# One-core language-model tower: the opening reordered, from the weight loads to the first attention heads

## The chip, the cores and the metric

The kernel runs on one core of a Trainium2 chip. The core has five engines that run side by side and meet only at semaphores: TensorE (PE in the rows, its weight loads PEld), VectorE (DVE), ScalarE (ACT), GpSimd (POOL) and SyncE (SP), which here only starts transfers. The metric is the device time of one execution in microseconds, the median of several runs. The kernel before took 1006.28 us (median of three, 1006.02 to 1006.45).

## The reference, cut to what matters

`x` holds 8 x 512 token ids below 2048. Everything is float32.

```python
h = gelu(codebook[x] @ W1 + b1) @ W2 + b2            # 256 -> 1024 -> 256
n = layernorm(h);  x_tok, x_pos = n[..., :128], n[..., 128:]
q, k, v = x_pos @ Wq, x_pos @ Wk, x_tok @ Wv         # 16 query heads, 4 key/value heads of 64
q = rotate(q, q_phase_angle)                         # one fixed angle for each head
att = q @ k^T / 8 + exp(alibi_log_slopes) * (i - j)  # causal
att = exp(att - max) / (1 + sum(exp(att - max)))
h = h + (att @ v) @ Wo
m = layernorm(h)
h = h + gelu((m @ U1) @ V1 + b1f) @ U2 @ V2 + b2f    # low rank 64
```

## The kernel before

**First stage, `token_table`.** The first expression depends on the token id alone. So it is computed once for each of the 2048 codebook rows, in four chunks of 512 (`NC = 4`), and kept in DRAM as a table of 640 columns: 256 of `h`, 128 of the normalised second half (the input of queries and keys), 256 of values. Each chunk is 8 steps; step n is numbered over all 32, `i` is the chunk and `m` the step in it. Every float32 matrix is split into a high and a low part, and a product is three matmuls. In a step TensorE makes `first_product(n)` (six matmuls of 512 columns) and `second_product(n - 2)` (twelve of 256). ScalarE does the gelu and the high part, VectorE the low part. `first_product(n)` needs the gelu of step n-2, and `second_product(n)` the low part of step n.

The order on every engine is written out by hand. At the start SP loads chunk 0 of the codebook, W1 in two halves of 128 rows (with the tiny `b1_col` between them), W2 in four parts, `b2_row`, and the other chunks. ScalarE makes the two high parts of W1, then two sines and an exponential (`sin_t`, `half`, `slope`), then meets the gelus. Its functions come in tables, and each change of function other than Copy is preceded by a load (ACT_TABLE_LOAD). VectorE prepares the angles (`ang`) ahead of the low parts of W1.

A chunk's rows are finished while the next one runs: `keep_rows` (VectorE, at m = 1) adds the bias into the tile `made`, `norm_front` (m = 2) takes the statistics, GpSimd raises to the power -1/2, `norm_back` (m = 4) writes the normalised columns of `made` and the normalised token half (`tokens`, in the buffer named scratch). TensorE turns those tokens (`turn_tokens`) at m = `TURN_AT` = 5, and multiplies them with Wv at m = 7. SP stores the rows twice: into `early_rows` (384 columns, for the first batch entry alone) and into `table`. The stage ends with a barrier of all engines once `early_rows` of the last chunk has landed.

**Second stage, `layer`.** It walks over 128 heads (8 batch entries of 16) in slots `s`, with 16 more slots to drain. At its head TensorE turns and multiplies the last chunk's tokens, and GpSimd gathers the first batch entry's rows from `early_rows` and, once the last values are stored, its values from `early_values`. The whole rows of batch entry b+1 are gathered from `table` by `gather(b + 1)` at slot 1 of entry b. Each gather is four indirect DMAs that GpSimd itself issues, before it goes on.

In a slot: TensorE makes the scores of head s in three units (`scores(s, 0..2)`: query block 3; 2 and 0; 1) into two PSUM banks taken in turn. VectorE adds the bias and takes the least (`least_of`, four instructions), ScalarE takes the exponentials (`exps`, four), VectorE takes the reciprocal of the sums (`invert`), GpSimd scales the probabilities (`normalize`, four instructions). Two slots later TensorE turns them (`turn`), ScalarE moves the turned tile to SBUF (`move`), and TensorE multiplies with the values for two heads at a time (`values`). Queries of two heads, keys of four and the inputs of the next batch entry are further products, listed by `first(s)`, and all go through one PSUM bank (`a_bank`) in turn: a product may start when VectorE has made the low part (`low`) of the one before. `first(s)` stands, on TensorE, between `scores(s, 1)` and `scores(s, 2)`; on ScalarE ahead of the exponentials of head s; on VectorE ahead of the fourth `least_of`. `second(s)` stands at the end of the slot on each of them.

## Time and profile before

| | |
|---|---|
| median of three runs | 1006.28 us |
| the profiled execution | 1006.18 us |
| its span in the trace | 1004.4 us |
| mean granted TensorE clock | 0.965 |
| PE / ACT / POOL / DVE busy | 87% / 72% / 63% / 61% |
| first stage, up to the barrier | about 0 to 126.8 us |
| first head's scores begin | 141.7 us |

The profiled execution lasted 1.8 us longer than its span, which is the time around the first and the last recorded instruction. TensorE is the busiest engine overall, but a share over the whole span says nothing of the opening; for that the trace is read stretch by stretch. Times of rows are microseconds from the start of the span.

### The profile page before, as it was taken

The page shows a single profiled execution, that of the slowest core. Times are in us where ns is not written, and L with a number is a line of the kernel's source. Part 1 is how long each engine was busy: PE and PEld are TensorE (multiplying, and loading weights), DVE is VectorE, ACT ScalarE, POOL GpSimd, SP SyncE. Part 2 cuts the span into 40 slices and gives each one's busy share as a digit, 9 for nine tenths or more (in the row PEclk, how much of TensorE's full clock was granted, in tenths as well). Part 3 has the DMA queues.
Part 4 walks back from the last instruction along what each step waited for, and adds up shares of the span by engine and source line. Part 5 has one row for each costly group of instructions (what it writes and reads, how often), then busy time and mean ns, then how long its engine had stood idle before and what let it go on. Part 6 is the DMA issues. An engine that isn't in the chain of part 4 may idle for free.

```text
span 1004.4 us, 16876 instructions
## 1 busy us (share of the span) xinstructions
PE 875.8 (87%) x5552; PEld 676.1 (67%) x5552; DVE 611.1 (61%) x1896; ACT 723.1 (72%) x1600; POOL 630.9 (63%) x600
## 2 busy tenths in 40 slices
PE   6999657999988998889888998899889988998876
PEld 5888545677865786568656875677567855786563
DVE  4565525777684658475847684767566765668321
ACT  6654236998678768886888687877787787868713
POOL 6000038999684878478857874887669775768520
PEclk9999867999999999999999999999999999999997
DMA  9232341001000200020001100010001000000000
GB/s 260 33 105 105 133 129 53 1 1 54 2 1 1 74 1 1 1 60 16 1 1 35 41 1 1 22 54 1 1 22 53 2 1 22 1 2 1 1 21 21
DMA packets 21206, 33.55 MB, mean 33 GB/s; under 512 B 2513, under 2 KB 18033, under 8 KB 21121
## 3 DMA queue, kind: packets, MB, share of 16 engines
q1 hardware_dynamic: 17360, 19.01, 5.8%
q0 software_dynamic: 3760, 13.48, 4.9%
q8 instruction: 45, 0.74, 0.3%
q14 instruction: 41, 0.33, 0.1%
HBM read 17.80 MB, written 14.68 MB: 32 GB/s over the span
## 4 chain that ended last, share of the span: by engine, by line
PE 51%; DVE 14%; ACT 12%; issue 8%; POOL 1%; DMA 0%; DVEq 0%; ACTq 0%; POOLq 0%
PE ps L972 15%; PE ps L1097 10%; PE ps L1081 8%; ACT probs L747 6%; PE ps L1069 5%; DVE probs L870 5%; PE ps L1070 4%; PE ps L1049 3%; ACT turned_sb L754 3%; PE ps L1043 2%; DVE q_both L887 1%; DVE xn L859 1%; PE ps L1044 1%; DVE sums L877 1%; ACT q_both L764 1%
## 5 line engine op out<-in xcount | busy, mean ns | idle before, releaser
L712 POOL TENSOR_SCALAR probs<-probs,sums 128x512 f32<-128x512 f32 (+3 forms) x512 | 546.4, 1085 | 200.7 <-DVE sums L879 200.3
L870 DVE CUSTOM_DVE_ANT_0 probs<-ps,causal,slope 128x512 f32<-128x512 f32 (+3 forms) x512 | 259.4, 547 | 81.0 <-PE ps L1070 79.1
L747 ACT ACTIVATE probs<-probs,least 128x512 f32<-128x512 f32 (+3 forms) x512 | 282.0, 553 | 23.3 <-DVE least L870 18.8
L754 ACT ACTIVATE turned_sb<-ps 128x1280 f32<-128x1280 f32 x128 | 157.4, 1230 | 89.4 <-PE ps L1081 89.4
L1069 PE MATMUL ps<-k_hi,q_both 128*128 128x512 f32 (+3 forms) x512 | 185.9, 363 | 33.4 <-DVE least L870 31.8
L1097 PE MATMUL ps<-turned_sb,token_rows 128*64 128x512 f32 (+3 forms) x1024 | 152.0, 438 | 29.6 <-ACT turned_sb L754 29.6
L1081 PE MATMUL ps<-ident,probs 128*128 128x128 f32 x1280 | 166.0, 278 | 4.0 <-POOL probs L712 4.0
L1070 PE MATMUL ps<-k_lo,q_both 128*128 128x512 f32 (+3 forms) x512 | 154.5, 327 | 0.0
L1097 PEld LDWEIGHTS ps<-turned_sb,token_rows 128*64 128x64 f32 x1024 | 74.7, 136 | 116.8 <-issue 100.4
L1081 PEld LDWEIGHTS ps<-ident,probs 128*128 128x128 f32 x1280 | 147.8, 144 | 7.0 <-POOL probs L712 5.4
L1069 PEld LDWEIGHTS ps<-k_hi,q_both 128*128 128x128 f32 x512 | 98.2, 192 | 78.8 <-DVE least L870 54.8
L1070 PEld LDWEIGHTS ps<-k_lo,q_both 128*128 128x128 f32 x512 | 98.9, 193 | 4.5
L747 ACT ACTIVATION_READ_ACCUMULATOR probs<-probs,least 128x1 f32 x512 | 96.1, 188 | 0.0
L887 DVE TENSOR_TENSOR q_both<-ps,q_both 64x512 fp32r<-64x512 f32 x128 | 88.1, 689 | 11.9 <-ACT q_both L764 8.7
L764 ACT ACTIVATE q_both<-ps 64x512 fp32r<-64x512 f32 x128 | 75.4, 589 | 23.6 <-PE ps L972 22.1
L251 POOL TENSOR_TENSOR row_guess<-row_var,row_power 128x4 f32<-128x4 f32 x4 | 4.1, 1026 | 97.0 <-DVE row_var L350 97.0
L972 PE MATMUL ps<-wo_lo,o_hi 128*128 128x256 f32 x224 | 63.3, 282 | 0.0
L972 PE MATMUL ps<-wo_hi,o_hi 128*128 128x256 f32 x224 | 63.2, 282 | 0.0
L972 PE MATMUL ps<-wo_hi,o_lo 128*128 128x256 f32 x224 | 62.9, 281 | 0.0
L922 DVE TENSOR_TENSOR o_lo<-ps,o_hi 128x512 fp32r<-128x512 f32 x64 | 44.2, 691 | 23.3 <-ACT o_hi L796 23.1
L913 DVE TENSOR_TENSOR y_lo<-ps,y_hi 128x512 fp32r<-128x512 f32 x8 | 5.5, 692 | 81.1 <-ACT y_hi L790 81.1
L786 ACT ACTIVATE ff<-ps,c_col 128x512 f32<-128x512 f32 x64 | 40.7, 685 | 18.0 <-PE ps L1044 17.9
(191 smaller groups left out, 1446.6 us busy)
## 6 DMA issues: line engine op xcount, KB each, us to landing
out_dram<-token_rows SPq DMA_DIRECT2D x7, 512.0 KB, 2.9
early_rows<-made SPq DMA_DIRECT2D x4, 768.0 KB, 3.6
token_table<-made SPq DMA_DIRECT2D x4, 768.0 KB, 5.3
rows<-in_L_tok_codebook_dram SPq DMA_DIRECT2D x4, 512.0 KB, 8.0
early_values<-xn SPq DMA_DIRECT2D x4, 512.0 KB, 3.0
token_table<-xn SPq DMA_DIRECT2D x4, 512.0 KB, 4.4
w_f<-in_L_tok_W_dram SPq DMA_DIRECT2D x2, 512.0 KB, 6.3
w_f<-in_L_tok_W_dram SPq DMA_DIRECT2D x4, 256.0 KB, 8.1
```

What stands on the lines that cost most here:

```text
L712: ins = pool.tensor_scalar(at, at, recip[:, s % P_RING, q:q + 1], None, ALU.mult)
L747: act.activation(at, at, ACT.Exp, bias=least[:, s % P_RING, q:q + 1], scale=-1.0, accum_out=sums[:, s % P_RING, q:q + 1]).then_inc(exped, 1)
L754: act.activation(turned_sb[:, s % 2, :], turn_ps, ACT.Copy).then_inc(moved, 1)
L764: act.activation(q_both[at, s % 4, :], a_of("q", n, 0)[at, :], ACT.Copy).then_inc(q_high, 1)
L870: dve.tensor_tensor_reduce(out=probs[:, s % P_RING, at], in0=bank(unit % 2)[:, UNIT_AT[q]:UNIT_AT[q] + P * (q + 1)], in1=causal[:, at], sc ...
L887: dve.tensor_tensor(q_both[to, s % 4, :], a_of("q", n, 0)[at, :], q_both[at, s % 4, :].bitcast(F32), ALU.subtract).then_inc(q_low, 1)
L922: dve.tensor_tensor(o_lo[:, p % O_RING, :], o_bank, o_hi[:, p % O_RING, :].bitcast(F32), ALU.subtract)\
L972: mm = pe.matmul(dst, w, x, start=n == 0, stop=n == len(parts) - 1)
L1069: pe.matmul(dst, w, k_hi[:, slot, 0:P * (q + 1)], start=True, stop=False)
L1070: mm = pe.matmul(dst, w, k_lo[:, slot, 0:P * (q + 1)], start=False, stop=True)
L1081: mm = pe.transpose(turn_ps[:, K_AT[k] + P * (q - k):K_AT[k] + P * (q - k + 1)], probs[:, s % P_RING, Q_AT[q] + P * k:Q_AT[q] + P * (k + 1 ...
L1097: mm = pe.matmul(o_bank[rows, P * k:T], v_rows[:, b % 3, k, n // REP * D:(n // REP + 1) * D], turned_sb[:, (s + e) % 2, K_AT[k]:K_AT[k] + ...
```

## The change

Six things are done. W1 is loaded and split in four parts, first the left 512 columns of both row halves, then the right 512. The preparation of the angles and the two sines and exponential move behind W1 (VectorE) and to step 5 (ScalarE). `turn_tokens` goes from m = 5 to m = 6. The store into `early_rows` becomes two, 256 columns when `keep_rows` is done and 128 when `norm_back` is. `gather(1)` is issued before the first `normalize`, and ScalarE takes one exponential of one column (`spare`) at the head of the second stage. For slots 0 and 1 the query and key products stand in `second(s)` instead of `first(s)`, and their low parts one slot later on VectorE.

```diff
-    TURN_AT, VALUES_AT = 5, 7
+    TURN_AT, VALUES_AT = 6, 7
...
+    def w1_part(n):
+
+        return n % KD, slice(n // KD * HID // 2, (n // KD + 1) * HID // 2)
...
-            for k in range(KD):
-                sp.dma_start(w1_f[:, k, :], g["W1"][k * P:(k + 1) * P, :]).then_inc(w1_in[k], 16)
-                if k == 0:
+            for n in range(2 * KD):
+                k, cols = w1_part(n)
+                sp.dma_start(w1_f[:, k, cols], g["W1"][k * P:(k + 1) * P, cols]).then_inc(w1_in[n], 16)
+                if n == 1:
                     sp.dma_start(b1_col[:, :], ...)
...
+                sp.wait_ge(row_kept, 2 * i + 2)
+                sp.dma_start(of_chunk(g["early_rows"])[:, :, 0:DIM], made[:, :, 0:DIM]).then_inc(early_in, 16)
                 sp.wait_ge(pos_normed, i + 1)
-                sp.dma_start(of_chunk(g["early_rows"]), made[:, :, :]).then_inc(early_in, 16)
+                sp.dma_start(of_chunk(g["early_rows"])[:, :, DIM:DIM + P], made[:, :, DIM:DIM + P]).then_inc(early_in, 16)
...
             for n in range(STEPS):
                 i, m = divmod(n, KH)
+                if n == 5:
+                    act.wait_ge(trig_in, 1)
+                    act.activation(sin_t[:, :], ang[:, :], ACT.Sin).then_inc(trig_out, 1)
+                    act.activation(half[:, :], ang[:, :], ACT.Sin, scale=0.5).then_inc(trig_out, 1)
+                    act.activation(slope[:, :], ls[:, :], ACT.Exp).then_inc(trig_out, 1)
...
-                    if n == 0:
-                        pe.wait_ge(w1_low, k + 1)
+                    if n == 0 or n == KH // 2:
+                        pe.wait_ge(w1_low, n // (KH // 2) * KD + k + 1)
...
+EARLY = 2
+def queries_and_keys(s):
...
 def first(s):
     i, j = divmod(s, HEADS)
-    out = []
-    if s % 2 == 0 and s // 2 + 1 < ALL // 2:
-        out.append(("q", s // 2 + 1, 0))
-    if s % 4 == 1 and (s + 3) // 4 < ALL // REP:
-        out.append(("k", (s + 3) // 4, 0))
+    out = [] if s < EARLY else queries_and_keys(s)
...
 def second(s):
-    out = []
+    out = queries_and_keys(s) if s < EARLY else []
...
             gather_first(slice(DIM + P, ROW), g["early_values"], first_values_in)
+            gather(1)
...
-                if i + 1 < B and j == 1:
+                if i >= 1 and i + 1 < B and j == 1:
                     gather(i + 1)
...
+            act.activation(spare[:, :], ident[:, 0:1], ACT.Exp)
             act.wait_ge(tok_full, 1)
...
+                if 1 <= s <= EARLY:
+                    for use in queries_and_keys(s - 1):
+                        low(*use)
                 for use in first(s):
                     low(*use)
```

ScalarE at the very start, before: the names w1_hi and w2_hi are high parts of the weights, hid the gelu's output, ang and ls the angles and log slopes.

```order
L280 ACTIVATE w1_hi<-w1_f 128x1024 [waits w1_in0]
L280 ACTIVATE w1_hi<-w1_f 128x1024 [waits w1_in1]
L282 ACT_TABLE_LOAD
L282 ACTIVATE sin_t<-ang 128x16 [waits trig_in]
L283 ACTIVATE half<-ang 128x16
L284 ACT_TABLE_LOAD
L284 ACTIVATE slope<-ls 128x16
L289 ACTIVATE w2_hi<-w2_f 128x512 [waits w2_in0]
L295 ACT_TABLE_LOAD [waits hid_full]
L295 ACTIVATE hid<-ps,b1_col 128x512 [waits b_in]
```

The same place in the changed kernel:

```order
L289 ACTIVATE w1_hi<-w1_f 128x512 [waits w1_in0]
L289 ACTIVATE w1_hi<-w1_f 128x512 [waits w1_in1]
L289 ACTIVATE w1_hi<-w1_f 128x512 [waits w1_in2]
L289 ACTIVATE w1_hi<-w1_f 128x512 [waits w1_in3]
L299 ACTIVATE w2_hi<-w2_f 128x512 [waits w2_in0]
L305 ACT_TABLE_LOAD [waits hid_full]
L305 ACTIVATE hid<-ps,b1_col 128x512 [waits b_in]
```

Two table loads and three small functions left this place. They stand ahead of the gelu of step 5 now, and a third load stands there too, since the gelu's table must come back.

GpSimd at the head of the second stage, before: token_rows are the gathered rows, probs the probabilities of a head.

```order
L717 DMA token_rows<-early_rows,idx 128x384 x4
L717 DMA token_rows<-early_values,idx 128x256 [waits values_in]
L717 DMA token_rows<-early_values,idx 128x256 x3
L712 TENSOR_SCALAR probs<-probs,sums 128x512 [waits recip_done,start]
L712 TENSOR_SCALAR probs<-probs,sums 128x384
L712 TENSOR_SCALAR probs<-probs,sums 128x128
L712 TENSOR_SCALAR probs<-probs,sums 128x256
L700 DMA token_rows<-token_table,idx 128x640 [waits right_in,left_in]
L700 DMA token_rows<-token_table,idx 128x640 x3
L712 TENSOR_SCALAR probs<-probs,sums 128x512 [waits recip_done]
```

And in the changed kernel:

```order
L736 DMA token_rows<-early_rows,idx 128x384 x4
L736 DMA token_rows<-early_values,idx 128x256 [waits values_in]
L736 DMA token_rows<-early_values,idx 128x256 x3
L719 DMA token_rows<-token_table,idx 128x640 [waits right_in,left_in]
L719 DMA token_rows<-token_table,idx 128x640 x3
L731 TENSOR_SCALAR probs<-probs,sums 128x512 [waits recip_done,start]
L731 TENSOR_SCALAR probs<-probs,sums 128x384
```

The four gathers of the second batch entry went from between the first and second head's scaling to ahead of both.

VectorE in the first heads, before: the ISA rows that write probs and least are `least_of`, q_both is the low part of two heads' queries, k_lo that of the keys, sums the reciprocal.

```order
L870 ISA probs,least<-ps,causal,slope 128x128 [waits scored]
L870 ISA least 128x1
L887 TENSOR_TENSOR q_both<-ps,q_both 64x512 [waits q_high] x2
L870 ISA probs,least<-ps,causal,slope 128x256 [waits scored]
L870 ISA least 128x1
L877 TENSOR_SCALAR sums<-sums 128x4 [waits exped]
L879 RECIPROCAL sums<-sums 128x4 [waits v_step]
L870 ISA probs,least<-ps,causal,slope 128x512 [waits scored]
```

And in the changed kernel, up to the query's low part, from the same `least_of` of head 0 on:

```order
L892 ISA probs,least<-ps,causal,slope 128x128 [waits scored]
L892 ISA least 128x1
L892 ISA probs,least<-ps,causal,slope 128x256 [waits scored]
L892 ISA least 128x1
L899 TENSOR_SCALAR sums<-sums 128x4 [waits exped]
L901 RECIPROCAL sums<-sums 128x4 [waits v_step]
L892 ISA probs,least<-ps,causal,slope 128x512 [waits scored]
L892 ISA least 128x1
L892 ISA probs,least<-ps,causal,slope 128x384 [waits scored]
...
L909 TENSOR_TENSOR q_both<-ps,q_both 64x512 [waits q_high] x2
```

The low part of the next queries went from ahead of head 0's fourth `least_of` to behind head 1's third. In the same way k_lo went from head 1's slot to behind the third `least_of` of head 2, where the low part of the queries after that follows it at once.

## Rows read from the trace of the kernel before

**Rows 1.** Stretch: us; busy of PE, PEld, DVE, ACT, POOL; granted clock; DMA share

```profile
16.80:116.80 100.00, 96.98 (x637) 87.07 (x636) 58.61 (x136) 55.30 (x88) 5.93 (x6) 1.00 0.35 100
```

**Rows 2.** Waits of TensorE from 16.8 to 116.8: us in total, times, longest

```profile
PE ps L495 <- DVE scratch L365: 2.6, 3, 0.9
```

**Rows 3.** Timeline of the start: start, us, instruction [idle before <-releaser]

```profile
6.97 0.94 SPq L194 DMA_DIRECT2D b_row<-in_L_tok_b_dram  x1
...
7.36 1.05 ACT L280 ACTIVATE w_hi<-w_f 128x1024 fp32r<-128x1024 f32 x1
9.90 1.06 ACT L280 ACTIVATE w_hi<-w_f 128x1024 fp32r<-128x1024 f32 x1 [1.49 <-DMA w_f<-in_L_tok_W_dram]
10.97 1.28 ACT L282 ACT_TABLE_LOAD   x1
...
15.95 0.69 ACT L295 ACTIVATE hid<-ps,b_col 128x512 f32<-128x512 f32 x1
...
7.50 0.69 DVE L324 TENSOR_TENSOR ct_lo<-ps,ct_hi 128x512 fp32r<-128x512 f32 x1 [0.16 <-ACT ct_hi L260]
...
10.18 2.35 DVE L385 TENSOR_TENSOR w_lo<-w_f,w_hi 128x1024 fp32r<-128x1024 f32 x2
...
11.55 0.77 PE L469 MATMUL ps<-ct_hi,w_hi 128*128 128x512 f32 x1 [4.72 <-DVE w_lo L385]
...
16.80 0.42 PE L469 MATMUL ps<-ct_hi,w_hi 128*128 128x512 f32 x1
```

**Rows 4.** DMA issues: out<-in, engine, count, KB each, us to landing

```profile
b_row<-in_L_tok_b_dram SPq DMA_DIRECT2D x1, 128.0 KB, 6.3
early_rows<-made SPq DMA_DIRECT2D x4, 768.0 KB, 3.6
early_values<-xn SPq DMA_DIRECT2D x4, 512.0 KB, 3.0
```

**Rows 5.** Timeline around step 5 of the first stage

```profile
27.75 0.69 ACT L295 ACTIVATE hid<-ps,b_col 128x512 f32<-128x512 f32 x1 [1.39 <-PE ps L471]
...
31.77 0.39 PE L469 MATMUL ps<-ct_hi,w_hi 128*128 128x512 f32 x1
```

**Rows 6.** Timeline of SP at the end of the first stage

```profile
122.73 0.36 SPq L200 DMA_DIRECT2D early_rows<-made  x1
```

**Rows 7.** Timeline of POOL and PE in the first heads

```profile
141.28 1.01 POOL L717 DMA_INDIRECT token_rows<-early_values,idx  x1 [0.30 <-issue]
151.09 4.29 POOL L712 TENSOR_SCALAR probs<-probs,sums 128x512 f32<-128x512 f32 x4 [8.79 <-DVE sums L879]
155.53 1.09 POOL L700 DMA_INDIRECT token_rows<-token_table,idx  x1 [0.15 <-issue]
...
160.62 12.76 POOL L712 TENSOR_SCALAR probs<-probs,sums 128x512 f32<-128x512 f32 x12
...
164.97 2.40 PE L1081 MATMUL ps<-ident,probs 128*128 128x128 f32 x10 [3.98 <-POOL probs L712]
```

**Rows 8.** Timeline of the first heads on DVE and ACT

```profile
142.95 0.75 DVE L870 CUSTOM_DVE_ANT_0 probs<-ps,causal,slope 128x512 f32<-128x512 f32 x1 [0.59 <-PE ps L1070]
...
150.34 0.18 DVE L879 RECIPROCAL sums<-sums 128x4 f32<-128x4 f32 x1
...
147.81 0.72 ACT L747 ACTIVATE probs<-probs,least 128x512 f32<-128x512 f32 x1
...
155.78 1.21 ACT L764 ACTIVATE q_both<-ps 64x512 fp32r<-64x512 f32 x2 [2.17 <-PE ps L972]
```

**Rows 9.** Stretches in the first heads, columns as in the first group

```profile
157.40:161.00 3.60, 1.97 (x10) 1.18 (x8) 2.54 (x10) 3.58 (x10) 2.96 (x4) 1.00 0.76 218
165.00:170.40 5.40, 5.40 (x19) 4.55 (x19) 1.66 (x6) 1.24 (x1) 5.40 (x5) 0.50 0.00 0
```

**Rows 10.** The page's groups of the whole run: busy, mean ns of one

```profile
L870 DVE CUSTOM_DVE_ANT_0 probs<-ps,causal,slope 128x512 f32<-128x512 f32 (+3 forms) x512 | 259.4, 547 | 81.0 <-PE ps L1070 79.1
L887 DVE TENSOR_TENSOR q_both<-ps,q_both 64x512 fp32r<-64x512 f32 x128 | 88.1, 689 | 11.9 <-ACT q_both L764 8.7
```

49 lines of the change are left out of this document (27 added, 22 removed).

## The prediction

> **What bounds the kernel now.** I read the stretches first, to learn where TensorE is full, then its waits, then the timeline of the two places where it is not. In the first stage, once running, TensorE is busy 96.98 of 100 us [rows 1]; what is saved ahead of it, or between its steps, is saved outright. What is left to take there is the late start at 11.55 [rows 3] and three waits of 2.6 us together for the tokens [rows 2]. At the end of that stage SP issues the last row store at 122.73 [rows 6], its landing takes 3.6 us [rows 4], and only then the barrier opens, at 126.8. In the second stage the first heads have an idle TensorE: its turn of head 1's probabilities starts at 164.97 after 3.98 us of waiting for GpSimd [rows 7]. Later the engines work in a fixed order with fixed work in each slot, so I carry every microsecond gained by slot 5 to the end.
>
> All sums are made against the profiled execution, 1006.18 us, which is 0.1 us under the median of 1006.28. About 0.2% (2 us) is what a measurement of this kernel can tell from no change.
>
> **First term, the start: 2.6 us.** Before, W1's first half was high-parted by ScalarE from 7.36 to 8.41, but VectorE began its low part only at 10.18, behind the preparation of the angles, and took 1.2 us for each half [rows 3]; TensorE began at 11.55. Now a part is 512 columns, half as many, so about 0.6 us on each. The two first parts together have the bytes of the old first half, which was in by 7.36 at the latest. ScalarE: 7.36 to 8.0. VectorE is free at 7.50 + 0.69 = 8.19 [rows 3], low part to 8.8. TensorE begins at 8.85, that is 2.7 us earlier; the second pair of parts of this product is ready at 9.4, before its first three matmuls end (12 matmuls took 16.80 - 11.55 = 5.25, so 0.44 each, 1.3 us for three). The right columns are needed first at step 4. The whole of W1 was in at 9.90 [rows 3], long before that.
>
> The next check is the gelu of step 0, since step 2's product started at 16.80 right behind it (15.95 + 0.69 = 16.64). Now the two products ahead end at 8.85 + 5.25 = 14.1. The first is complete at about 11.7, the gelu's table load takes 1.28 and ends at 13.0. The gelu also waits for `b2_row`, issued at 6.97 and 6.3 us under way [rows 3, 4], so landed at 13.3; gelu to 14.0, product of step 2 at 14.1. So TensorE stays 2.7 us early, with 0.1 us of cover. SP issues two more transfers ahead of `b2_row` now, which can take back a little: I take 2.6. Lower bound: if `b2_row` lands 1.5 us later (two issues at up to 0.94 us, the longest single issue in [rows 3]), 1.2. Upper bound 2.9.
>
> The three small functions with their loads are not removed. Before, they and the gelu's load stood between 10.97 and 15.95 together with one 0.6 us weight part, so the block is 15.95 - 10.97 - 0.6 = 4.4 us, and all of it stands ahead of the gelu of step 5 now. ScalarE is idle there from 27.75 - 1.39 = 26.36 [rows 5]. So in before's times the block ends at 30.7 and the gelu at 31.4, where it was 28.4. The product that needs it is that of step 7, started at 31.77 [rows 5]: 0.3 us of cover. The low part is ready 1.4 us after the gelu, 32.8, for `second_product(5)`, which stands behind 1.4 us of step 7's product, 33.2. Later steps give back 1.39 us of lag each. Cost 0, with cover of 0.3 us; upper bound below.
>
> The Trainium skill (ScalarE: Activation LUTs, What ACT_TABLE_LOAD costs) says that each switch of table costs about 2.66 us, the load of 1283 ns and a drain of 1380 ns. The trace shows the load, 1.28 us, and no drain: the load stands at 10.97, at once behind the weight part of 9.90 + 1.06 = 10.96 [rows 3]. By the page's figure the block would be about 8.5 us, an estimate, and the sum some 4 us worse.
>
> **Second term, the tokens: 2.6 us.** Moved by one step of 2.8 us, `turn_tokens` finds its input there long since: the three waits of up to 0.9 us each, 2.6 in all [rows 2], go. What it feeds is ScalarE's high part, VectorE's low part (0.6 and 0.7) and the value products behind the next step's 2.8 us of matmuls, so nothing is late in its place. Bounds 2.2 to 2.7.
>
> **Third term, the last store: 1.2 us.** 256 of the 384 columns go out when `keep_rows` is done, some 5 us before 122.73. The 128 left are 256 KB. The rows give 768 KB in 3.6 and 512 KB in 3.0 [rows 4], 0.6 us for each 256 KB, so 2.4 for 256 KB: 1.2 us earlier. The pieces are shorter (512 bytes instead of 1536), and no row shows such a store; if it takes as long as the 512 KB one, 3.0, the gain is 0.6. Upper bound 1.5. The SP queue holds nothing in front of the early store that is later than before.
>
> ScalarE's exponential at the head of the second stage needs a load of 1.28 [rows 3] and itself, while TensorE turns the last tokens; I take it that the values come about 0.3 us later. They wait for nobody but GpSimd's value gathers. These set the next term.
>
> **Fourth term, the first heads: 5.9 us.** I walk in before's times. GpSimd is free at 141.28 + 1.01 = 142.3, now 142.6. The four gathers take 160.62 - 155.53 = 5.1 us [rows 7], so they end at 147.9. Is head 0's reciprocal there? Its first `least_of` ends at 143.70 [rows 8]. The exponentials started at 147.81, behind ScalarE's high parts of the next queries (1.21) and a table load; now both are gone from there, and they start at 143.75. The four took from 147.81 to 150.1, 2.3 us (the reciprocal followed at 150.34), and now end at 146.1. The reciprocal is 4.0 us early, at 146.5. So `normalize(0)` starts at 147.9 instead of 151.09, 3.2 early, bounded by the gathers, and ends at 152.2. `normalize(1)` follows at 152.2 instead of 160.62, since the gathers are no longer between, and ends at 156.5 instead of 164.9.
>
> Then the gain is cut. The second query product writes the bank of the first keys, whose low part now stands behind head 2's first three `least_of`. These begin when head 1's reciprocal is done, 151.5, and take three times about 0.5 (the group's mean is 547 ns), then 0.7 for the keys' low part (as a low part of queries, 689 ns, [rows 10]): 153.8. TensorE makes the queries until about 155.2, ScalarE takes their high part at 155.3 to 155.5, where it was 155.78 [rows 8]. So heads 2 and 3 come only 0.3 us earlier. The gain arrives at the turn of head 1: instead of 164.97 it starts behind head 3's scores, at 161.0 - 0.3 = 160.7. That is 4.3 us. GpSimd has finished at 156.5, with 4 us of cover.
>
> The clock adds to it. From 165.0 to 170.4, behind that wait, TensorE was busy throughout at a granted clock of 0.50, which is 1.2 GHz; from 157.4 to 161.0, ahead of it, it was 1.00 [rows 9], 2.4 GHz. If it doesn't fall, the 5.4 us shrink to about 2.7. I take six tenths of that, 1.6: 4.3 + 1.6 = 5.9. If the clock falls as before, 4.3 to 5; if it never falls, 7 to 8. If it also stays at 0.50 where it was 1.00 before, the 1.97 us busy of 157.4 to 161.0 double [rows 9], and 4.3 - 2.0 = 2.3 is left, or 2.0 with the first products of head 1: the lower bound.
>
> **Sum.** 2.6 + 2.6 + 1.2 + 5.9 = 12.3. 1006.2 - 12.3 = 993.9 us.
>
> **The rivals.**
>
> *The clock stays low through the first heads.* For it: the clock was 0.50 from 165.0 to 170.4 although TensorE was busy all that time [rows 9]. Against: the wait before that stretch goes. Price: the fourth term is 2.0 to 3.5, so 996.3 to 997.8.
>
> *The start is held by a later landing.* `b2_row` or a part of W1 lands late, because ten transfers are issued ahead of `b2_row` instead of eight, in one queue. Price: the first term 1.2 or less, 995.3 to 996.5.
>
> *The block at step 5 is not covered.* Cover is 0.3 us. If each of three loads took twice its 1.28, the block is 3.8 us longer, and 3.5 us come back: 997.4. By the page above, this is what would happen.
>
> *The moved gathers do nothing.* The turn of head 1 could wait for another thing than GpSimd, say for the turned tile or for a low part. Then the fourth term is 0 to 1: 998.8 to 999.8. Against it stands the single releaser of those 3.98 us [rows 7].
>
> *Slower than before.* The first stage's TensorE could run at the low clock longer, since it starts sooner after less work and with its steps spread. At the low clock a matmul of 512 columns starts every 0.44 us, behind 16.80 one every 0.23. A step of 2.8 us would take about 5.2, 2.4 more. The gain of 12.3 is used up after five steps and it is slower by over 2 us after six, that is with the low clock until some 45 us. Against it: the start has the same matmuls in the same order with no gap that the old one lacked.
>
> **How the numbers follow.** Forecast, 991.0 to 996.2: 0.62. Clock low: 0.14. Late landing: 0.08. Block not covered: 0.05. Gathers nothing: 0.05. Slower: 0.02. Below 991: 0.04. The forecast's own range is the likeliest sum with the fourth term anywhere from 4.3 to 8 and the others near their values. The range for 8 in 10 must reach over the clock and the landing cases, to 998.0, and takes in the block case, whose price lies between: 991.0 to 998.0, which leaves out 0.11. Faster by over 0.2% (below 1004.2) holds all cases but the last, and a hundredth for something unseen: 0.97; within 0.2%: 0.01; slower: 0.02.
>
> **What would show it.** First term: the first product's first matmul at 8.8 to 9.0, the first gelu at 13.3. Second: no wait of the token turn for scratch. Step 5: three table loads near 24, and no TensorE wait there. Third: the second early store lands about 2.4 us after its issue. Fourth: `normalize` of head 0 at once behind the gathers, no wait of a turn for GpSimd, granted clock 1.00 behind head 4's scores. What would make it wrong: a first gelu later than 14.5, a token-turn wait that has moved to the value products, a granted clock of 0.50 beyond the fourth head, or a wait in the second stage that returns what was gained.

## The result, and the profile after

The changed kernel takes 987.75 us (median of six runs, 986.64 to 991.27) where the one before takes 1004.68 beside it (median of six, 1000.61 to 1006.45). The ratio is 0.9841, with a 95% interval of 0.9814 to 0.9868: 16.9 us faster. The forecast was 12.3 us, 993.9, and its range ended at 991.0.

The profiled execution of after took 987.25 us, with a span of 985.4 us and a mean granted clock of 0.977 (before 0.965). First the waits of TensorE in the first stage (0 to 110 us; total, times, longest):

```profile
PE ps L467 <- DMA rows<-in_L_tok_codebook_dram: 5.0, 1, 5.0
PE ps L480 <- DVE w_lo L390: 2.1, 1, 2.1
PE ps L480 <- ACT hid L305: 0.4, 1, 0.4
PE ps L495 <- DVE made L347: 0.3, 2, 0.2
```

The three waits for scratch [rows 2] are gone. Behind the first product there is a wait of 0.4 us for the gelu of step 0, and two for `made` with 0.3 us together, which stood in before too. The timeline of the start shows where the first comes from:

```profile
12.17 1.28 ACT L305 ACT_TABLE_LOAD   x1
14.12 0.69 ACT L305 ACTIVATE hid<-ps,b_col 128x512 f32<-128x512 f32 x1 [0.66 <-DMA b_row<-in_L_tok_b_dram]
9.04 0.77 PE L480 MATMUL ps<-ct_hi,w_hi 128*128 128x512 f32 x1 [2.10 <-DVE w_lo L390]
14.86 0.56 PE L480 MATMUL ps<-ct_hi,w_hi 128*128 128x512 f32 x1 [0.35 <-ACT hid L305]
```

TensorE begins at 9.04 instead of 11.55 [rows 3]. The table is loaded at 13.45, but the gelu stands until 14.12 for the landing of `b2_row`, and the product of step 2 starts at 14.86, where it was 16.80. Of the 2.5 us, 1.94 arrive.

ScalarE at step 5, where the sines and the exponential now stand (start, us):

```profile
24.54 1.28 ACT L294 ACT_TABLE_LOAD   x1
25.83 0.22 ACT L294 ACTIVATE sin_t<-ang 128x16 f32<-128x16 f32 x1
26.17 1.28 ACT L296 ACT_TABLE_LOAD   x1
27.70 1.28 ACT L305 ACT_TABLE_LOAD   x1
29.00 0.69 ACT L305 ACTIVATE hid<-ps,b_col 128x512 f32<-128x512 f32 x1
```

The block is 29.00 - 24.54 = 4.46 us long, each step follows the last at once, and no wait of TensorE for `hid` lies there. The store at the end, as SP issues its two parts:

```profile
112.56 0.36 SPq L206 DMA_DIRECT2D early_rows<-made  x1
117.65 0.36 SPq L208 DMA_DIRECT2D early_rows<-made  x1
```

What each of the two took (KB, us from issue to landing):

```profile
early_rows<-made SPq DMA_DIRECT2D x1, 512.0 KB, 3.7
early_rows<-made SPq DMA_DIRECT2D x1, 256.0 KB, 2.3
```

The 512 KB went out 5.1 us ahead, the 256 KB landed in 2.3 us, and TensorE begins its second stage at 120.48, 2.83 us after the issue where it was 126.84 - 122.73 = 4.11.

The first heads on GpSimd, ScalarE and TensorE:

```profile
140.07 1.01 POOL L719 DMA_INDIRECT token_rows<-token_table,idx  x1 [0.30 <-issue]
141.12 8.52 POOL L731 TENSOR_SCALAR probs<-probs,sums 128x512 f32<-128x512 f32 x8
```

```profile
142.89 0.50 PE L998 MATMUL ps<-pos_hi,wk_hi 128*128 128x512 f32 x1 [1.74 <-DVE q_both L909]
146.62 0.50 PE L998 MATMUL ps<-pos_hi,wq_hi 128*128 128x512 f32 x1 [1.77 <-DVE k_lo L913]
147.65 1.25 PE L1110 MATMUL ps<-ident,probs 128*128 128x128 f32 x10
152.66 1.26 PE L1110 MATMUL ps<-ident,probs 128*128 128x128 f32 x10
```

```profile
147.62 1.21 ACT L784 ACTIVATE q_both<-ps 64x512 fp32r<-64x512 f32 x2 [2.99 <-PE ps L998]
161.54 0.60 ACT L789 ACTIVATE k_hi<-ps 128x512 fp32r<-128x512 f32 x1 [0.48 <-PE ps L998]
```

GpSimd scales heads 0 and 1 in one run right behind the last gather, and both turns start without a wait for it. The turn of head 1 is at 152.66 instead of 164.97 [rows 7]. Two new waits stand in TensorE, 1.74 and 1.77 us: keys behind queries, and queries behind keys, in the shared bank. Stretches (us; busy of PE, PEld, DVE, ACT, POOL; clock; DMA share):

```profile
14.80:111.60 96.80, 96.30 (x636) 87.13 (x636) 58.52 (x136) 59.60 (x95) 8.84 (x10) 1.00 0.38 110
135.50:141.70 6.20, 3.95 (x19) 3.12 (x19) 4.88 (x18) 4.55 (x13) 4.94 (x6) 1.00 0.62 174
141.70:147.90 6.20, 3.24 (x17) 2.73 (x18) 4.10 (x13) 2.21 (x8) 6.20 (x6) 1.00 0.20 69
147.90:154.00 6.10, 3.95 (x30) 3.33 (x29) 4.14 (x14) 6.02 (x17) 4.08 (x5) 1.00 0.00 0
154.00:161.50 7.50, 7.31 (x48) 5.50 (x47) 5.81 (x18) 6.99 (x17) 7.17 (x8) 1.00 0.01 2
```

In the three stretches from 135.5 to 154.0 TensorE is less than two thirds busy, and the granted clock is 1.00 (2.4 GHz) in them as in the other two. Before, the heads, of which [rows 9] show two pieces alone, read:

```profile
141.69:155.97 14.28, 11.03 (x33) 8.35 (x34) 8.91 (x30) 7.94 (x21) 5.33 (x6) 0.62 0.07 19
155.97:164.97 9.00, 3.40 (x20) 2.62 (x19) 4.62 (x16) 6.71 (x19) 8.05 (x9) 0.88 0.51 147
164.97:176.15 11.18, 11.18 (x57) 8.55 (x58) 5.37 (x16) 6.44 (x13) 9.22 (x9) 0.76 0.00 0
```

So the low clock before was not a matter of 165 to 170.4 alone. Its mean was 0.62 from the first scores to the turn of head 0.

To compare kernels, four marks of the trace are used below: the product of step 2; the last store's issue into `early_rows`; the first scores; and the high part of the third keys (`k_hi`), which ends the first heads. "Heads" is the time between the last two, "rest" the time from there to the span's end. The rest holds some short spells in which the granted clock falls to 0.50 (last section); their number stands in the last column. Each row is one profiled execution, and spans are known to 0.1 us.

| kernel | step 2 | last store | first scores | turns of heads 0, 1 | heads | rest | spells |
|---|---|---|---|---|---|---|---|
| before | 16.80 | 122.73 | 141.69 | 155.97, 164.97 | 34.46 | 828.3 | 4 |
| after | 14.86 | 117.65 | 135.50 | 147.65, 152.66 | 26.04 | 823.9 | 2 |
| x_start | 17.08 | 119.83 | 137.61 | 149.87, 154.86 | 26.13 | 823.8 | 2 |
| x_turn | 15.05 | 121.03 | 138.86 | 152.72, 157.72 | 27.76 | 823.7 | 2 |
| x_store | 14.46 | 117.11 | 135.76 | 149.78, 155.03 | 29.2 | 824.7 | 2 |
| x_gather | 15.94 | 118.68 | 136.52 | 150.28, 155.86 | 28.01 | 823.9 | 2 |
| x_order | 14.09 | 117.01 | 134.83 | 145.45, 149.99 | 24.05 | 826.0 | 3 |
| x_heads_back | 14.34 | 117.09 | 135.07 | 148.92, 158.26 | 33.67 | 824.1 | 2 |
| x_only_heads | 16.15 | 122.08 | 141.12 | 153.16, 158.17 | 25.94 | 824.1 | 2 |
| x_before_fill | 16.86 | 122.82 | 141.85 | 156.14, 165.16 | 31.96 | 826.7 | 3 |
| x_bsplit | 14.15 | 117.45 | 135.26 | 146.68, 151.54 | 25.15 | 829.5 | 5 |
| x_warm | 14.12 | 117.20 | 134.69 | 146.11, 150.96 | 25.16 | 825.2 | 3 |
| x_nospare | 14.59 | 117.33 | 134.87 | 149.15, 154.00 | 28.01 | 826.8 | 4 |
| x_keys | 14.09 | 117.14 | 135.00 | 145.15, 150.28 | 25.49 | 827.1 | 4 |
| y_before | 18.03 | 123.92 | 142.71 | 156.99, 165.99 | 34.48 | 827.9 | 4 |
| y_after | 15.22 | 117.97 | 135.37 | 148.94, 153.80 | 27.31 | 825.5 | 3 |
| y_before_warm | 17.41 | 123.42 | 141.23 | 153.95, 162.94 | 31.99 | 828.6 | 4 |

### The profile page after: what moved, and what is told of

Read it like the earlier page. It is cut to its first block, busy times and chain, and to the rows that moved or that the text cites. A ratio compares the mean times of both kernels' runs of the same rounds, so it can differ in the third digit from the quotient of the medians.

```text
span 985.4 us, 16889 instructions
## 1 busy us (share of the span) xinstructions
PE 864.0 (88%) x5552; PEld 667.6 (68%) x5552; DVE 612.3 (62%) x1898; ACT 724.5 (74%) x1604; POOL 630.6 (64%) x600
## 4 chain that ended last, share of the span: by engine, by line
PE 49%; DVE 18%; ACT 13%; issue 8%; POOL 0%; DMA 0%; DVEq 0%; ACTq 0%; POOLq 0%
PE ps L998 15%; PE ps L1126 10%; PE ps L1110 7%; ACT probs L767 6%; DVE probs L892 6%; PE ps L1098 5%; PE ps L1099 4%; PE ps L1078 3%; ACT turned_sb L774 3%; DVE q_both L909 2%; PE ps L1072 2%; DVE sums L899 2%; DVE o_lo L944 1%; DVE xn L881 1%; PE ps L1073 1%
## 5 line engine op out<-in xcount | busy, mean ns | idle before, releaser
L774 ACT ACTIVATE turned_sb<-ps 128x1280 f32<-128x1280 f32 x128 | 157.4, 1229 | 81.8 <-PE ps L1110 81.7
L1098 PE MATMUL ps<-k_hi,q_both 128*128 128x512 f32 (+3 forms) x512 | 183.6, 359 | 32.8 <-DVE least L892 29.9
L1110 PE MATMUL ps<-ident,probs 128*128 128x128 f32 x1280 | 163.1, 275 | 0.1
L1099 PE MATMUL ps<-k_lo,q_both 128*128 128x512 f32 (+3 forms) x512 | 152.4, 323 | 0.0
L1110 PEld LDWEIGHTS ps<-ident,probs 128*128 128x128 f32 x1280 | 144.9, 142 | 2.6 <-POOL probs L731 1.3
L909 DVE TENSOR_TENSOR q_both<-ps,q_both 64x512 fp32r<-64x512 f32 x128 | 88.1, 688 | 10.2 <-ACT q_both L784 6.9
L899 DVE TENSOR_SCALAR sums<-sums 128x4 f32<-128x4 f32 x128 | 34.4, 269 | 32.5 <-ACT probs L767 32.2
```

What stands on the lines that cost most here:

```text
L774: act.activation(turned_sb[:, s % 2, :], turn_ps, ACT.Copy).then_inc(moved, 1)
L899: step(dve.tensor_scalar(recip[:, s % P_RING, :], sums[:, s % P_RING, :], 1.0, None, ALU.add))
L909: dve.tensor_tensor(q_both[to, s % 4, :], a_of("q", n, 0)[at, :], q_both[at, s % 4, :].bitcast(F32), ALU.subtract).then_inc(q_low, 1)
L1098: pe.matmul(dst, w, k_hi[:, slot, 0:P * (q + 1)], start=True, stop=False)
L1099: mm = pe.matmul(dst, w, k_lo[:, slot, 0:P * (q + 1)], start=False, stop=True)
L1110: mm = pe.transpose(turn_ps[:, K_AT[k] + P * (q - k):K_AT[k] + P * (q - k + 1)], probs[:, s % P_RING, Q_AT[q] + P * k:Q_AT[q] + P * (k + 1 ...
```

## The experiments

The theory is that of the prediction: four separate gains, the last one from GpSimd's gathers moved out of the way and a clock that stays up. Its rivals here: the gain of the heads is the clock alone; it comes from the new order of queries and keys; and what was gained beyond the forecast lies outside the opening. The median and the ratio to before (95% interval) stand with each. The runs were made in five groups, and the kernel before, timed beside each, had medians of 1004.68 (the result), 1006.28 (x_start to x_gather), 1004.84 (x_order to x_before_fill), 1006.59 (x_bsplit to x_keys) and 1005.34 us (the y runs). So a difference of two medians from different groups is uncertain by up to 2 us; the marks within a trace are not touched by this. Nothing is left out of the computation in any of them.

**x_start.** W1 in two halves and the sines early again, all else as after.

```diff
-            for n in range(2 * KD):
-                k, cols = w1_part(n)
+            for k in range(KD):
...
-                if n == 5:
-                    act.wait_ge(trig_in, 1)
```

> The changed kernel with the start put back: W1 in two halves, angles, sines and exponential ahead of the gelus. Theory 1 (the start is worth what its milestone shows and nothing absorbs it): the product of step 2 starts at 16.8 again instead of 14.86, and the run is 1.9 us longer than the changed kernel. Theory 2 (as put on record): 2.6 us. Rival (something later waits for another thing): under 0.5 us. A difference of over 3 us would have to come from the clock later on.

Measured: 990.14 us, 0.985 (0.9827 to 0.9873). Step 2's product comes 17.08 - 14.86 = 2.2 us later, and it is still 2.1 to 2.2 later at the last store and the first scores. So nothing behind it absorbs the first term. Its size, 2.2 between these two executions, varies: the old start has step 2 at 16.15 to 18.03 in its six, the new one at 14.09 to 15.94 in its eleven.

**x_turn.** `turn_tokens` back at m = 5.

```diff
-    TURN_AT, VALUES_AT = 6, 7
+    TURN_AT, VALUES_AT = 5, 7
```

> The changed kernel with the tokens turned at step 5 of a chunk again. Theory 1 (milestones: the stage between step 2's product and the last store was 3.1 us shorter): 3.1 us longer, all of it before the last store. Theory 2 (only the three waits): 2.6 us. Rival: nothing, if the wait has moved to the value products.

Measured: 992.91 us, 0.9875 (0.9853 to 0.9898). Its waits for scratch are back:

```profile
PE ps L506 <- DVE scratch L375: 2.5, 3, 0.9
```

From step 2 to the last store it takes 105.98 us, after 102.79: 3.19 us, more than the 2.5 of idle. The reason can be seen at one of the three turns, in before and then in after:

```profile
105.11 0.28 PE L486 MATMUL ps<-w_hi,hid_lo 128*128 128x256 f32 x1
106.24 0.66 PE L495 MATMUL ps<-ident,scratch 128*128 128x128 f32 x4 [0.85 <-DVE scratch L365]
```

```profile
103.90 0.28 PE L497 MATMUL ps<-w_hi,hid_lo 128*128 128x256 f32 x1
104.02 0.60 PE L506 MATMUL ps<-ident,scratch 128*128 128x128 f32 x4
```

From the start of the last matmul to that of the turn it is 1.13 us with the wait and 0.12 without. The matmul records overlap (0.28 long, the next 0.12 behind), and a wait takes that overlap too: 1.0 us where the row says 0.85. Three times 1.0 is nearly the 3.1 to 3.2. Part of this may lie in the record alone, since the ends of matmuls are modelled; the starts are what count.

**x_store.** One store of 384 columns again.

```diff
-                sp.wait_ge(row_kept, 2 * i + 2)
-                sp.dma_start(of_chunk(g["early_rows"])[:, :, 0:DIM], made[:, :, 0:DIM]).then_inc(early_in, 16)
```

> The changed kernel with one store of early_rows for a chunk. Both theories: last store issue to first instruction of the second stage 4.1 us instead of 2.8, so 1.3 us longer. Rival (short pieces cost as much as they save): 0.3 or less.

Measured: 991.48 us, 0.9854 (0.9829 to 0.988). From the last store's issue to TensorE's second stage it takes 121.19 - 117.11 = 4.08 us, after 2.83: 1.25. The median is 3.7 above that of after, more than the 1.25, but the two come from different groups: by the ratios, 0.9854 and 0.9841, it is 1.3. The profiled execution also shows 29.2 us of heads against 26.04, with a clock of 0.70 up to head 0's turn where after has 1.00. This edit changes nothing there, and after itself has 0.70 there in its second profile (y_after), so I put it to the clock of that execution.

**x_gather.** The second batch entry's gather back in slot 1, between the two `normalize`; the new order of queries and keys stays.

```diff
-            gather(1)
...
-                if i >= 1 and i + 1 < B and j == 1:
+                if i + 1 < B and j == 1:
```

> The changed kernel with the second batch entry's gathers back behind the first head's scaling. Theory stall (GpSimd's time alone): head 1's scaling ends at about 154.1 instead of 149.6, its turn comes 1.4 us later than at 152.66, so 1.4 us longer. Theory clock (a TensorE that waits there falls to 0.50 and does the next 5 us at half pace): 3 to 5 us longer, with a granted clock of 0.50 in the stretch behind the turn.

Measured: 990.19 us, 0.9852 (0.9824 to 0.988). GpSimd:

```profile
141.96 4.29 POOL L731 TENSOR_SCALAR probs<-probs,sums 128x512 f32<-128x512 f32 x4 [5.12 <-DVE sums L900]
146.41 1.09 POOL L719 DMA_INDIRECT token_rows<-token_table,idx  x1 [0.16 <-issue]
151.51 17.02 POOL L731 TENSOR_SCALAR probs<-probs,sums 128x512 f32<-128x512 f32 x16
```

Head 0 is scaled before the gathers, so head 1 is ready at 155.8. Head 1's turn is 5.58 us behind head 0's, where it was 9.00 before. So with the reordered queries alone most of the gap goes already, since head 0's exponentials no longer stand behind the next queries; a wait of 0.4 us for GpSimd is left at a turn. Behind head 0's turn the clock is 1.00, so the theory of a fall there is out. Heads are 28.01 us, 2.0 more than after: 0.6 between the two turns, and 1.6 ahead of head 0's, where the clock was 0.73.

**x_order.** The gathers stay early, the queries and keys go back to `first(s)`.

```diff
-EARLY = 2
+EARLY = 0
```

> The changed kernel with the queries and keys of slots 0 and 1 in their old places; the gathers and the extra exponential stay early. From the first head's scores to the high part of the third keys took 34.5 us before and 26.0 in the changed kernel, 28.0 with the gathers put back. Theory either (each of the two moves takes away the wait for GpSimd, so one is enough): 26 to 28.5, and 0 to 2.5 us more than the changed kernel in all. Rival (the order of products is what gained): over 30, and 4 us more or worse.

Measured: 987.87 us, 0.9831 (0.9803 to 0.9859). Heads 24.05 us, 2 us less than after, with the clock at 1.00 in both:

```profile
134.80:146.00 11.20, 8.10 (x39) 5.71 (x40) 8.92 (x31) 7.41 (x21) 9.31 (x10) 1.00 0.45 134
146.00:158.90 12.90, 10.96 (x71) 8.20 (x69) 10.14 (x30) 12.30 (x32) 12.57 (x13) 1.00 0.00 1
```

So with the gathers early the new order is not needed, and in the opening it costs 2 us, 1.5 of them ahead of head 0's turn, where after has the waits of 1.74 and 1.77 us for the shared bank. The medians don't show it (987.87 and 987.75): this execution has one spell of low clock more in the rest, 2.1 us.

**x_heads_back.** Both together, and `spare` with them: the second stage as before, the first as after.

```diff
-EARLY = 2
+EARLY = 0
...
-            gather(1)
...
-            act.activation(spare[:, :], ident[:, 0:1], ACT.Exp)
```

> The changed kernel with all of the second stage put back: old places of queries and keys, gathers behind the first head's scaling, no extra exponential. Theory stall only: the stretch is 30.5 to 31, 4.3 to 5 us longer than the changed kernel. Theory stall and clock: 33 to 35, 7 to 8.5 us longer, with the wait of 4 us for GpSimd and a granted clock of 0.50 behind it.

Measured: 995.6 us, 0.9909 (0.9877 to 0.994), 7.9 above after. The wait for GpSimd is back, as long as in [rows 7]:

```profile
158.26 1.97 PE L1108 MATMUL ps<-ident,probs 128*128 128x128 f32 x8 [4.18 <-POOL probs L731]
```

Heads 33.67 us. The clock was 0.64 up to head 0's turn and 0.81 behind head 1's, so this is the theory of stall and clock (33 to 35), not that of the stall alone (30.5 to 31). The rest has 2 spells and 824.1 us, as in after, so in this execution it does not follow the order of the first heads.

**x_only_heads.** The opposite: the first stage as before (W1 in halves, turn at 5, one store), the second as after.

```diff
-    TURN_AT, VALUES_AT = 6, 7
+    TURN_AT, VALUES_AT = 5, 7
...
-            for n in range(2 * KD):
+            for k in range(KD):
...
-                sp.wait_ge(row_kept, 2 * i + 2)
```

> The opposite: start, token turn and store as before, the second stage as changed. Theory (terms add up): the stretch of the first heads is 26 to 28 us as in the changed kernel, and the run 6.4 us longer than the changed kernel, about 994. Rival (the first heads' gain hung on when the stage began): the stretch is above 30.

Measured: 996.41 us, 0.9914 (0.9887 to 0.9942). First scores 141.12, as before; heads 25.94 us, as after. The two halves of the change are worth about the same. By the ratios the first stage is worth 7.3 us and the second 6.8; by the medians 996.41 - 987.75 = 8.7 and 995.6 - 987.75 = 7.9, against 16.9 for both. In the traces the first scores come 141.12 - 135.50 = 5.6 us later in this kernel (forecast 6.4 in all), and the heads are 33.67 - 26.04 = 7.6 us longer in x_heads_back. So the halves add up to within what the groups and the clock scatter, not closer.

**x_before_fill.** The kernel before, with twelve more matmuls ahead of the turn of head 1, into columns that nothing reads.

```diff
             def turn(s):
+                if s == 1:
+                    pe.wait_ge(moved, 1)
+                    for _ in range(12):
+                        pe.matmul(bank(4)[:, 256:512], g["wq_hi"][:, 0:P], g["wq_hi"][:, 0:256], start=True, stop=True,
+                                  skip_group_check=True)
                 pe.wait_ge(normed, s + 1)
```

> The kernel before with twelve extra matmuls of 256 columns between the first turned tile's move and the turn of head 1, where TensorE waits 4 us for GpSimd; their result goes to an unused part of a bank. They fit in the wait even at 1.2 GHz (12 x 0.21 = 2.6 us). Theory clock (a TensorE at work doesn't fall to 0.50 there): the wait stays, the turn starts when GpSimd is done, and the stretch behind it takes 2.5 to 3 us less. Theory stall only: no difference from the kernel before.

Measured: 1003.11 us, 0.9982 (0.9963 to 1.0001). TensorE:

```profile
160.99 1.58 PE L1077 MATMUL ps<-wq_hi 128*128 128x256 f32 x12
165.16 1.31 PE L1086 MATMUL ps<-ident,probs 128*128 128x128 f32 x10 [2.59 <-POOL probs L712]
```

The turn comes when it came before and still waits for GpSimd, but its ten matmuls take 1.31 us instead of 2.40 [rows 7], and the clock stays 1.00 behind it: heads 31.96 instead of 34.46. That is the clock's share behind the turn, 2.5 us, with the turn at its old time (23.3 us behind the first scores in both). The change brought 8.4, so the clock behind the turn is not its cause alone; the clock ahead of head 0's turn was low here too (0.74), and this run does not test it. The median is 1.7 us below the one beside it, and its interval reaches 1.

**x_bsplit.** After with the old order of queries (`EARLY = 0`), and a semaphore of its own for `b2_row`, which VectorE waits for in `keep_rows`; the gelu waits for `b1_col` alone.

```diff
-                    act.wait_ge(b_in, 32)
+                    act.wait_ge(b_in, 16)
...
                     if n == 0:
+                        dve.wait_ge(b2_in, 16)
                         dve.wait_ge(row_half, i + 1)
```

> Old places of queries and keys, the rest of the change kept (984.9 us span last time), and the first gelu waits for b1 alone; b2 gets a semaphore of its own, waited for by the first kept rows. In the changed kernel the first gelu waited 0.66 us for b2's landing and TensorE 0.35 us behind it. Theory: the product of step 2 starts 0.3 to 0.9 us sooner after the first matmul (5.1 to 5.3 us after it instead of 5.8), 0.3 to 0.7 us in all. Rival: nothing, since the next parts of W2 are waited for instead.

Measured: 989.01 us, 0.982 (0.9799 to 0.9842). ScalarE:

```profile
12.12 1.28 ACT L305 ACT_TABLE_LOAD   x1
13.41 0.69 ACT L305 ACTIVATE hid<-ps,b_col 128x512 f32<-128x512 f32 x1
```

The gelu follows its table at once, and step 2's product starts 5.3 us behind the first one, as expected. It starts at 14.15, 14.12 and 14.09 in the three kernels that have this edit (x_bsplit, x_warm, x_keys). In the eight profiled executions that have the new start without it, it starts between 14.09 and 15.94 (x_order and x_gather): in x_order the gelu waits for nothing, and in x_gather it waits longest.

```profile
15.20 0.69 ACT L305 ACTIVATE hid<-ps,b_col 128x512 f32<-128x512 f32 x1 [2.10 <-DMA b_row<-in_L_tok_b_dram]
```

So the landing of `b2_row` costs from nothing to 1.8 us at the start, by the execution.

**x_warm.** As x_bsplit, with unread matmuls in the gaps of TensorE: 34 behind the first stage, 5 and 12 in the second stage's opening, 4 and 6 between its products.

```diff
+            for _ in range(34):
+                pe.matmul(bank(0), w1_hi[:, 0, 0:P], w1_hi[:, 0, 0:512], start=True, stop=True, skip_group_check=True)
```

> The same with 61 matmuls whose result nobody reads: 34 behind the last product of the first stage, the others in TensorE's waits up to the first scores. Theory clock (work keeps the granted clock at 1.00): no 0.50 from the stages' border to the first scores, the transposes and products there take half, 1.5 to 3 us from the second stage's begin to the first scores less than 15.0. Rival (the fillers are in the way): the barrier or the first scores come later, by up to 2 us.

Measured: 986.48 us, 0.9803 (0.9783 to 0.9823). The clock holds through the border, and then falls all the same:

```profile
120.00:134.70 14.70, 10.86 (x54) 8.11 (x54) 2.79 (x5) 5.54 (x9) 8.14 (x9) 1.00 0.58 180
134.70:147.00 12.30, 9.73 (x38) 7.50 (x39) 9.23 (x31) 7.38 (x21) 10.41 (x11) 0.78 0.40 121
```

From TensorE's start in the second stage to the first scores it takes 14.66 us, where after takes 15.02 at a clock of 0.50 up to 134.5. The 1.5 to 3 us expected are not there: TensorE's own speed hardly counts in this stretch. The longest wait in it is for gathered rows (2.27 us here, 2.45 in after). This is the lowest median of all, but its interval and that of after (0.9814 to 0.9868) overlap, so it is not shown to be faster.

**x_nospare.** As x_order, without the spare exponential.

```diff
-            act.activation(spare[:, :], ident[:, 0:1], ACT.Exp)
```

> Old places of queries and keys and early gathers, without the extra exponential. The table load of 1.28 us comes back ahead of the first exponentials. Theory path (head 0's exponentials are on the chain to the turn of head 0): the stretch from first scores to third keys is 1.3 us longer than 24.05. Theory gathers (GpSimd isn't free before the gathers end anyway): under 0.5 us.

Measured: 989.28 us, 0.983 (0.9809 to 0.9851). The table load of 1.28 us stands at 139.70 again, right ahead of head 0's exponentials. Heads 28.01 against 24.05, but up to head 0's turn the clock was 0.62 here and 1.00 there, so the 4 us can't be put down to the load, and what it costs by itself stays open. The kernel before, with the same order and load and the same clock of 0.62, also takes 14.28 us up to head 0's turn, and with the gathers early head 1's turn comes 4.85 us behind it instead of 9.00.

**x_keys.** After as it is, with x_bsplit's semaphore and the keys of heads 4 to 7 in the values' bank instead of the shared one.

```diff
-    home = {("x", 0, 0): c_bank, ("q", 0, 0): bank(4)}
+    home = {("x", 0, 0): c_bank, ("q", 0, 0): bank(4), ("k", 1, 0): o_bank}
```

> The changed kernel's order of queries and keys, with the second keys in the values' bank, so that neither they nor the third queries wait for a low part in the shared bank (1.74 and 1.77 us of waits in the changed kernel), and the split bias semaphore. Theory bank (the shared bank is what makes the new order slower): the stretch goes from 26.0 to 24.0 or less. Rival (the place on VectorE and ScalarE is what costs): 25.5 to 26.

Measured: 987.58 us, 0.9808 (0.9784 to 0.9832). The turn of head 0 comes 10.15 us behind the first scores instead of 12.15, and both waits of TensorE in the shared bank are gone; heads 25.49 us, where 24.0 or less was expected. Up to head 0's turn this is as short as x_order (10.62), so the two waits are what the new order costs there. Behind head 1's turn it takes 10.2 us at a clock of 0.83, where after takes 8.9 at 1.00; that is 1.3 us, and without them the heads would be 24.2, an estimate. As a whole the kernel is not told apart from after.

**y_before, y_after.** The two kernels once more, unchanged, for a second profile of each.

> The kernel before once more, for its clock. Theory luck (where the clock falls differs from execution to execution, and each fall in the long middle costs 1.2 to 1.6 us): the stretch of the first heads is again 33 to 35, and from the third keys to the end it is 823.8 us plus about 1.3 for each low spell seen (828.2 with four last time). Rival (the old opening brings the four spells): four again.

> The changed kernel once more. Theory luck: the stretch of the first heads is 26 to 28, by how long the clock is at 0.50 in it, and the rest 823.8 plus 1.3 for each spell beyond two. Rival: 26.0 and two spells again.

Measured, one run each: 1006.93 and 989.98 us. Opening of before: the same within 0.1 in the heads (34.48). Of after: heads 27.31 against 26.04, since the clock was 0.72 in places where it had been 1.00 (0.70 in the whole of the 13.57 us up to head 0's turn):

```profile
135.40:141.50 6.10, 5.36 (x19) 4.36 (x19) 4.61 (x17) 4.49 (x13) 4.84 (x6) 0.72 0.60 167
141.50:147.50 6.00, 2.93 (x10) 2.45 (x11) 4.62 (x13) 2.04 (x7) 6.00 (x6) 0.72 0.25 92
```

Spells in the rest: 4 and 3. In four profiled executions the two kernels differ by two spells and by one, where they run the same program.

**y_before_warm.** The kernel before with the unread matmuls of x_before_fill and x_warm, to see whether a warmer opening leads to fewer spells in the rest.

> The kernel before with the same 61 unread matmuls around the stages' border, and the twelve in the wait for GpSimd. If the clock stays at 1.00 through the first heads, what remains of the 34.5 us is waiting alone. By the record's own split (4.3 waiting, the rest clock) the stretch is 30 to 31; by theory GpSimd only, with a faster TensorE waiting longer in the same place, it is 32 or more.

Measured: 1002.24 us (ten runs, 999.49 to 1007.3), 0.9985 (0.9959 to 1.0011). The clock did not stay up: its mean was 0.68 from the first scores to head 0's turn and 0.83 behind head 1's, although the twelve matmuls stood ahead of it. So the split of waiting and clock that the run was made for is not had from it. Heads are 31.99 as in x_before_fill, but by other parts: 12.72 us up to head 0's turn (there 14.29) and 10.28 from head 1's turn on (there 8.65). Unread matmuls do not always hold the clock. The rest is 828.6 us with 4 spells, as before, and so does not follow TensorE's work at the border of the stages.

## Why the prediction was right in its mechanisms and wrong in its sum

| term | forecast | measured, first pair | second pair (y) |
|---|---|---|---|
| start, at step 2's product | 2.6 | 1.94 | 2.81 |
| tokens, step 2 to last store | 2.6 | 3.14 | 3.14 |
| last store, issue to stage 2 | 1.2 | 1.28 | 1.28 |
| stage 2's start to first scores | 0 | -0.17 | 0.11 |
| first heads, scores to third keys | 5.9 | 8.42 | 7.17 |
| the rest | 0 | 4.4 | 2.4 |
| sum | 12.3 | 19.0 | 16.9 |

**First term.** TensorE at 9.04 (forecast 8.8 to 9.0), gelu at 14.12 instead of 13.3. The cover of 0.1 us that I gave it was not there: the landing of `b2_row` held the gelu for 0.66 us. That is the rival of the late landing, at half its price here (0 to 1.8 us over eight executions), and x_bsplit removes it.

**Step 5.** Three loads, 4.46 us for the block (forecast 4.4), no wait of TensorE. The Trainium skill (ScalarE: Activation LUTs, What ACT_TABLE_LOAD costs) gives 2.66 us for each switch of table; this case's trace has 1.28 for each of three, one straight behind the other's function.

**Second term.** The waits went whole and moved nowhere. The step that was mis-sized is "the three waits of up to 0.9 us each, 2.6 in all": a wait costs 1.0 where its row says 0.85, so 3.1.

**Third term.** 2.3 us to land, forecast 2.4; 1.28 us gained, and x_store says 1.25.

**Fourth term, the largest miss inside the opening.** It has two parts. GpSimd's part was right in kind: `normalize` of head 0 right behind the gathers, no turn that waits for GpSimd. The step that failed is "ScalarE takes their high part at 155.3 to 155.5, where it was 155.78. So heads 2 and 3 come only 0.3 us earlier". Counted from the first scores, 155.78 is 14.1 us, and after it is 147.62 - 135.50 = 12.1: 2.0 us earlier, not 0.3. My walk used before's durations up to there, and these were taken at a clock of 0.62, which I had not read: I read it for 157.4 to 161.0 and 165.0 to 170.4 alone [rows 9]. The second profile of the same program bears this out: y_after, at 0.70, takes 13.57 us to head 0's turn, only 0.7 less than before, and after, at 1.00, takes 12.15. The product of those queries took 1.0 us in after (146.62 to 147.62), not 1.4, and the low part of the keys ahead of it ended about 1 us sooner. So the turn of head 1 came 6.1 us earlier (2.13 up to head 0's turn, 3.99 from there), where I had 4.3. The other 2.3 us lie behind it, where I took "six tenths" of 2.7: in the first pair the clock did not fall there at all. x_before_fill puts the share of the clock behind that turn at 2.5 with the waits in place. Between it and after are 31.96 - 26.04 = 5.9 us more: 2.1 ahead of head 0's turn, where the clock differs too (0.74 and 1.00), and 4.0 between the turns, where the wait for GpSimd went. Which edit brings it: each of the two, the gathers and the new order, ends the wait for GpSimd or all but 0.4 us of it (x_order 24.05, x_gather 28.01, both undone 33.67); together they are no better than the gathers alone.

**"I carry every microsecond gained by slot 5 to the end."** The work does carry: less 1.6 us for each spell, the rest is 820.4 to 822.2 us in all 17 profiled executions. But it was 4.4 us shorter in the first pair and 2.4 in the second, most of it the spells (4 and 2, 4 and 3). The step that failed here is "the engines work in a fixed order with fixed work in each slot": the work is fixed, its time is not. The forecast had no term for it, and the range allowed nothing for what the clock does from one execution to the next. By the medians 16.9 us were gained. The opening accounts for 14.6 of them by the first pair and 14.5 by the second, so some 2.4 are the rest's. Whether the change has a part in that is open. All seven executions with 2 spells have the new first or second stage, and none of the four with both stages as before; but six with both stages changed have 3 to 5, and no edit here sets the number. Besides, with 1.6 us taken off for each spell, the four with both stages as before have 821.5 to 822.2 and the thirteen others 820.4 to 821.5. That is about 1 us which goes with the change, and no run shows where it lies.

**Rivals.** The clock stayed up through the heads in the first pair, and only in part in the second (0.70 up to head 0's turn), so that it did was luck; the late landing came half true; the block at step 5 was covered; the gathers did something. Slower: the clock was 1.00 from 15 to 114 us.

With all that the first pair measured in the opening the sum is 14.6 and the time 1006.2 - 14.6 = 991.6, still 3.8 us above the median. The rest's 2.3 is one part of this. The other 1.5 is where the forecast started: it was taken from 1006.18, and the kernel before had a median of 1004.68 beside the result. As a gain, 16.9 stands against the forecast's 12.3.

## What to carry to other kernels

Before a gain is walked through with durations from a trace, read the granted clock of every stretch from which they come. Where it is low, as the 0.62 here, the durations hold for that clock alone; the changed kernel may run there at another, and one and the same kernel had 1.00 in one execution and 0.70 in the next. Count a wait of TensorE between dense matmuls as its idle time and the lost overlap, here 1.0 us for a row of 0.85. When two edits both remove the same wait, try each alone: the second here costs 2 us in the opening, since it brings two waits for a shared PSUM bank, and gives nothing. Look also at what TensorE did right ahead of each fall of the clock, in stretches of a few microseconds, before calling it chance.

## What the runs showed of the hardware

The clock falls to 0.50 for short spells in the long middle of the kernel, and each fall stands behind a wait of TensorE. In wide stretches this can't be seen, since TensorE is busy for 293.64 of the 322.50 us from 161.5 to 484.0 in after. After, around its first spell, in short ones (columns as above):

```profile
482.50:486.00 3.50, 1.53 (x10) 1.25 (x9) 3.45 (x11) 2.03 (x4) 3.16 (x3) 1.00 0.00 0
486.00:489.50 3.50, 3.50 (x15) 3.07 (x14) 1.04 (x3) 1.85 (x8) 2.89 (x4) 0.51 0.00 0
```

Ahead of the spell TensorE is busy for 1.53 of 3.5 us, at a clock of 1.00; in the spell it is busy throughout, at 0.51. What it waits for is a bank of scores that VectorE frees. VectorE is at the low parts of two other products then and comes to its `least_of` late:

```profile
484.82 0.39 PE L1098 MATMUL ps<-k_hi,q_both 128*128 128x256 f32 x1 [1.97 <-DVE least L892]
```

This wait of 1.94 to 1.98 us comes once in each batch entry but the first, 119 times in the 17 profiled executions. All 51 spells begin with its end or up to 1.5 us behind it, and none stands elsewhere between the heads and the drain, which begins at some 950 us. But 68 of the waits have no spell behind them, and they look the same. The next one in after, then the stretches ahead of its end and behind:

```profile
589.75 0.39 PE L1098 MATMUL ps<-k_hi,q_both 128*128 128x256 f32 x1 [1.97 <-DVE least L892]
587.40:591.00 3.60, 1.63 (x10) 1.33 (x9) 3.47 (x11) 2.13 (x5) 3.26 (x3) 1.00 0.00 0
591.00:594.40 3.40, 3.40 (x22) 2.75 (x20) 1.76 (x6) 2.75 (x8) 3.02 (x4) 1.00 0.00 0
```

So the wait goes with the fall, and what picks one wait and not the next is not found. No run takes the wait away, so that the spells would go with it is not shown. It is the next thing to try: by these rows it costs 2 us in each of seven batch entries, and the falls behind it another 1.6 us each.

A batch entry with such a spell takes some 104.9 us from wait to wait, one without 103.3. The number of spells goes from 2 to 5 in the profiled executions, with the same program in the rest. It is worth up to 5 us, or 0.5%, more than the effect of several of the edits here.
